# Attention with relative positions and a feed-forward layer on one core: the order of a unit's matmuls, and two orders of transfers

## What is computed

```
x = L0_attn_q                                  # 8 x 1024 x 256, 16 heads of 16
qkv = q @ in_proj_weight.T + in_proj_bias
scores = jnp.einsum('bhid,bhjd->bhij', qh, kh)
rel = jnp.clip(pos[None, :] - pos[:, None], -K, K) + K          # K = 64
bias_r = jnp.einsum('bhid,rd->bhir', qh, rel_pe)
bias = jnp.take_along_axis(bias_r, rel, axis=-1)
attn = jax.nn.softmax(scores + bias, axis=-1)
out = jnp.einsum('bhij,bhjd->bhid', attn, vh)   # then @ out_w.T + out_b
x = _layernorm(x + attention)
x = _layernorm(x + ffn(x))   # gelu(x @ bw1.T + b1) @ bw2.T + b2, hidden 1024, binarized weights
```

## Time and profile before

| | |
|---|---|
| median of 3 runs | 2308.47 us (2308.45 to 2308.74) |
| the profiled execution | 2306.05 us, its span 2304.1 us |
| busy share of the span | PE 96%, DVE 76%, ACT 68%, POOL 47% |
| granted TensorE clock | 0.982 of full speed over the span |
| projections; attention; feed-forward | about 0 to 219 us; 219 to 1960 us; 1961 to 2304 us |

### The profile page before, as it was taken

One profiled execution on the slowest core, in us unless ns is written; L12 is line 12 of the kernel. 1 busy time (PEld: TensorE's weight loads), 2 busy tenths in 40 slices (PEclk: granted clock), 3 DMA queues, 4 the chain that ended last, 5 costly groups with the idle time before them and its releaser, 6 DMA issues. The chain is left out here.

```text
span 2304.1 us, 47825 instructions
## 1 busy us (share of the span) xinstructions
PE 2213.8 (96%) x14580; PEld 1261.2 (55%) x14580; DVE 1740.0 (76%) x3447; ACT 1566.1 (68%) x2192; POOL 1086.9 (47%) x1803
## 2 busy tenths in 40 slices
PE   8997799999999999999999999999999999899997
PEld 5554355545555555555555555555555544788886
DVE  3444688888888888888888888888888884788885
ACT  3444277777777777777777777777777776577676
POOL 1000444555445554455554555545555442577763
PEclk9998599999999999999999999999999999999999
DMA  9997877777777777777777777777777771433321
GB/s 305 402 334 273 215 215 212 219 210 212 218 213 221 207 215 219 211 218 207 215 220 211 220 206 215 220 213 216 208 215 218 215 214 49 122 100 109 108 66 46
DMA packets 334570, 468.55 MB, mean 203 GB/s; under 512 B 89797, under 2 KB 262550, under 8 KB 334486
## 3 DMA queue, kind: packets, MB, share of 16 engines
q0 software_dynamic: 120960, 215.78, 34.6%
q1 hardware_dynamic: 204358, 243.32, 33.0%
q10 hardware_dynamic: 9168, 8.52, 1.1%
HBM read 244.73 MB, written 221.25 MB: 202 GB/s over the span
## 5 line engine op out<-in xcount | busy, mean ns | idle before, releaser
L1025 ACT ACTIVATE probs<-weigh_ps 128x1024 f32<-128x1024 f32 x1024 | 1047.7, 1023 | 197.3 <-PE weigh_ps L1203 188.6
L1164 PE MATMUL ring_ps<-keys,queries 48*128 48x512 f32 x2048 | 853.8, 478 | 22.0 <-DVE partial_max L1068 13.7
L1079 DVE CUSTOM_DVE_ANT_1 ring_ps<-ring_ps,band_all 128x512 f32<-128x512 f32 x1008 | 681.2, 715 | 213.6 <-PE ring_ps L1164 213.4
L1203 PE MATMUL weigh_ps<-queries,keys 50*128 50x512 f32 (+3 forms) x2688 | 748.1, 383 | 0.0
L1068 DVE TENSOR_REDUCE partial_max<-ring_ps 128x2 f32<-128x1024 f32 x512 | 627.7, 1226 | 116.2 <-PE ring_ps L1164 88.5
L1164 PEld LDWEIGHTS ring_ps<-keys,queries 48*128 48x128 f32 x2048 | 369.9, 187 | 511.7 <-issue 371.8
L1220 PE MATMUL sum_ps<-probs,values 128*32 128x512 f32 x4096 | 546.4, 605 | 0.1
L1014 ACT ACTIVATE carried<-weigh_ps 128x260 f32<-128x260 f32 (+1 forms) x512 | 211.9, 414 | 255.4 <-PE weigh_ps L1153 255.4
L925 POOL COPY carried<-carried 128x252 f32<-128x252 f32 x430 | 159.1, 395 | 458.1 <-ACT carried L1014 458.1
L1188 PE MATMUL weigh_ps<-ident,band_all 128*128 128x128 f32 x2048 | 362.5, 289 | 1.5 <-ACT carried L1014 0.6
L1203 PEld LDWEIGHTS weigh_ps<-queries,keys 50*128 50x128 f32 x2688 | 357.6, 186 | 10.4 <-issue 5.9
(11 more groups left out here) (131 smaller groups left out, 1852.9 us busy)
## 6 DMA issues: line engine op xcount, KB each, us to landing
band_scr<-carried SPq DMA_DIRECT2D x256, 512.0 KB, 6.0
band_all<-band_scr POOLq DMA_DIRECT2D x128, 512.0 KB, 5.4
band_all<-band_scr POOLq DMA_DIRECT2D x128, 256.0 KB, 4.5
keys<-k_scr POOLq DMA_DIRECT2D x128, 240.0 KB, 8.1
k_scr<-k_parts SPq DMA_DIRECT2D x16, 1792.0 KB, 9.8
queries<-q_scr POOLq DMA_DIRECT2D x128, 128.0 KB, 3.8
o_scr<-weighted_s SPq DMA_DIRECT2D x64, 256.0 KB, 8.2
keys<-k_scr POOLq DMA_DIRECT2D x128, 120.0 KB, 5.2
```

Source lines behind the costliest of these rows:

```text
L1025: nc.scalar.activation(probs[:, u % PROBS], weigh_ps[weigh_of["scores", at]][:], ACT.Exp).then_inc(s_pr, 1)
L1079: nc.vector.tensor_tensor_reduce(out=both, in0=both, in1=bias, scale=1.0, scalar=LOWEST, op0=ALU.add, op1=ALU.max, accum_out=partial_max[: ...
L1164: nc.tensor.matmul(dst, query_rows(c, h, ROWS, tile * P, (tile + 1) * P), key_rows(c, h, ROWS, c0, c0 + 512), start=True, stop=True, tile_ ...
L1203: last = nc.tensor.matmul(weigh_ps[weigh_of["scores", at]][:, h, e0 * P:e1 * P], key_rows(c, h, QROWS, k0, k0 + P), query_rows(c, h, QROWS ...
```

## The change

Three edits. In `products`, the two weighing products of a unit are written first and both looks behind them (before: look, weighing, weighing, look). In the attention stage SP's two transfers of ones are moved from the head of its program to behind the first four band writes. In the feed-forward stage, for tiles 2 and 3, SP issues the inverse ahead of the heads and the residual, and POOL's first operations are in another order.

```
-                sp.wait_ge(s_set, 5)
-                for h in range(HG):
-                    row = keys[h * ROW_TILE + ROWS:h * ROW_TILE + QROWS].bitcast(F32)
-                    sp.dma_start(...).then_inc(s_one, 16)
                 for step in range(-START, FIRST):
                     for u in range(UNITS):
+                        if step == 1 - START and u == NT:
+                            sp.wait_ge(s_set, 5)
+                            for h in range(HG):
+                                row = keys[h * ROW_TILE + ROWS:h * ROW_TILE + QROWS].bitcast(F32)
+                                sp.dma_start(...).then_inc(s_one, 16)
                         unit(0, step, u)
...
-                    if looked:
-                        look(i, n, first)
                     if step >= 0:
                         weigh(step, m, part, 1 - first)
                         weigh(step, m, part, first)
                     if looked:
+                        look(i, n, first)
                         look(i, n, 1 - first)
...
-                    if it >= 2 * EARLY:
+                    if it < 2 * EARLY:
+                        spread_inverse(sp, it, inverse_wide)
+                    else:
                         load_sums(sp, it)
                     load_heads(sp, it, heads_raw)
                     load_residual(sp, it, x_in)
                     if it >= 2 * EARLY:
                         write_inverse(sp, it)
-                    spread_inverse(sp, it, inverse_wide)
+                        spread_inverse(sp, it, inverse_wide)
...
+                skip(0)
                 divide(2)
                 residual(2)
-                skip(0)
+                divide(3)
+                skip(1)
                 for it in range(IT + 2):
                     if 0 <= it - 2:
                         add_skip(it - 2)
-                    if it + 1 < IT:
+                    if 0 < it and it + 1 < IT:
                         skip(it + 1)
-                    if it + 3 < IT:
+                    if 0 < it and it + 3 < IT:
                         divide(it + 3)
```

More of the change, by code:

```diff
@@ L835, in unit @@
                             write_bands(i, chunk)
-                sp.wait_ge(s_set, 5)
-                for h in range(HG):
-                    row = keys[h * ROW_TILE + ROWS:h * ROW_TILE + QROWS].bitcast(F32)
-                    sp.dma_start(flat(row, 0, [row.ap[0], [P, SLOTS * KCOLS // P], [1, P]]),
-                                 flat(ones[:], 0, [ones[:].ap[0], [0, SLOTS * KCOLS // P], [1, P]])
-                                 ).then_inc(s_one, 16)
                 for step in range(-START, FIRST):
                     for u in range(UNITS):
+                        if step == 1 - START and u == NT:
+                            sp.wait_ge(s_set, 5)
+                            for h in range(HG):
+                                row = keys[h * ROW_TILE + ROWS:h * ROW_TILE + QROWS].bitcast(F32)
+                                sp.dma_start(flat(row, 0, [row.ap[0], [P, SLOTS * KCOLS // P], [1, P]]),
+                                             flat(ones[:], 0, [ones[:].ap[0], [0, SLOTS * KCOLS // P], [1, P]])
+                                             ).then_inc(s_one, 16)
                         unit(0, step, u)
```

## The result

The changed kernel takes 2324.91 us (median of 4 runs, 2321.16 to 2327.96), the kernel before 2308.6 (4 runs, 2308.45 to 2309.71): ratio 1.007, 95% interval 1.0055 to 1.0085. It is slower, by 16.3 us. The forecast was 2340, with 2318 to 2358 as the range. The profiled execution is 2326.46 us, its span 2324.6, so between the two profiles the span grew by 20.5 us.

| us | before | after | difference | of this part |
|---|---|---|---|---|
| VectorE's first reduction | 239.73 | 237.52 | -2.2 | -2.2 |
| TensorE's first load of step 0 | 274.42 | 272.22 | -2.2 | 0 |
| of step 1 | 305.27 | 304.06 | -1.2 | +1.0 |
| of step 63 | 1931.01 | 1955.46 | +24.45 | +25.7 |
| feed-forward stage, first matmul | 1961.03 | 1985.48 | +24.45 | 0 |

What follows compares the result with a forecast made beforehand. The prediction took a ring between TensorE and VectorE, each waiting for the other, to bound the kernel. 2306.05 + 44 (edit 1) - 7 (edit 2) - 5 (edit 3) = 2338, or 2340 us as median; range 2318 to 2358.

Steps and rivals of the forecast that it cites:

- VectorE's late start on odd looks: Attention steps, edit 1: odd first looks end 0.25 us late per pair, lengthening the step 0.5 to 1.0 us; chance 0.63.
- more idle time in all: Profile from 600 to 1800 us: ScalarE's exponentials start earlier after TensorE, with more idle time in all.
- 0.7 us a step: Edit 1's lengthening of each attention step; in 62.5 steps +44 us, bounds +22 and +62.
- the forecast's own 0.5 to 1.0: Likeliest case: the attention step lengthens by 0.5 to 1.0 us, giving 2328 to 2358 us; chance 0.63.
- half is taken up: Rival 2: idle times re-arrange, leaving 0.35 us a step or less, 2318 and down to 2313 us; chance 0.17.
- the unrounded 0.86: Delay left per step after idle time ahead of VectorE's eight reductions covers part of 0.25 us each; taken as 0.7.
- VectorE's ring is the longer one at those same places: Reason for counting at zero the relief of the band product's wait for ScalarE, 0.32 us a step, 20 us at most.
- a later reduction holds the next odd unit's second look: Ring between TensorE and VectorE: TensorE waits for the delayed reduction, 0.05 us to spare; two of eight pairs excepted.
- The rule that I gave for the rival: Rival 3, TensorE bound, 2284 or 2287 us, chance 0.14: holds if looks load 0.25 us or more after a reduction's end.
- an unchanged 5.8: Edit 2, attention start: 5.8 us from POOL's band read issue to VectorE's first reduction, then 6.5 us earlier.
- the divide can begin some 3 us sooner: Edit 3, feed-forward start: without residual and heads ahead of the inverse, TensorE's 3.38 us wait goes almost wholly.
- what might hold it back: Edit 3's gain, taken as -5 us: VectorE's L1442, 1769 ns on average beside busy POOL, whose work now comes earlier.

Runs made afterwards that it cites:

- even and odd units apart: Kernel before with the new products order in only even units: 2307.23 against 2306.8 us, ratio 1.0003; in only odd units: 2343.17 us, ratio 1.0145.
- the short odd operation: VectorE's operation on odd looks reads 256 of 512 columns per head: 2308.11 us on the kernel before, 2282.37 us with edit 1 in all units.
- the two other kernels with this edit: Kernel before with edit 2 alone: 2304.44 us, ratio 0.9985; kernel before with edits 2 and 3: 2300.86 us, ratio 0.9971.
- the transfers alone: Kernel before with only SyncE's part of edit 3, the inverse ahead of heads and residual: 2307.16 against 2307.03 us, ratio 0.9999.
- GpSimd's order alone: Kernel before with only GpSimd's part of edit 3, first skip foremost, divide of tile 3 before the second skip: 2302.73 us, ratio 0.998.
- Two kernels that shorten one suspect each: VectorE reads half the columns, old and new order: even-look reduction 2284.0 and 2328.95 us; odd-look operation 2308.11 and 2282.37 us.

## Why the prediction was right, and what was off

**The sign and where the loss begins: right.** The loss is edit 1's, in every steady step, through VectorE's late start on odd looks: shown by the edit alone (+24.4 us), by even and odd units apart, and by the short odd operation, which turns the loss into a gain. VectorE's wait per pair was forecast at about 0.65 and came to 0.61, that before the reductions at nearly none (0.33 us a step). ScalarE was forecast to have "more idle time in all", and it has (busy 144.84 of 200 us, was 147.50). Ahead of its exponentials its idle time fell, from 129.9 to 68.3 us; ahead of the band copies its wait for the band product rose, from 184.4 to 262.2. The band product's wait and its row are gone as forecast.

**The size: 0.7 us a step was taken, 0.41 measured** (+44 against +25.7; the bounds were +22 and +62). That lies between the forecast's own 0.5 to 1.0 and the 0.35 of the rival "half is taken up", and 2325 us lies in the stated range but below the forecast's 2328 to 2358. Of 2.00 us of delay a step 1.14 was to be taken up; VectorE's waits show 1.56, and 1.16 taken up. These two figures say where the time went and not why, since VectorE's work is unchanged and they must differ by the lengthening of the step. The delay itself stands in the traces: from the first weight load of an odd unit to VectorE's start on its first look it is 0.69 us before and 0.92 to 0.93 after, in each of the eight pairs (means of steps 8 to 50). So the look is 0.23 us late where 0.25 was taken, and that is 0.15 of the 0.45 us between the unrounded 0.86 and the 0.41. VectorE's wait grew by 0.195 only, so TensorE reaches an odd unit some 0.035 us sooner after VectorE than before, 0.28 a step, and this term was put at zero. The band product's wait that went is of that size, 0.32 us a step or 0.04 a pair, and I had dropped it because "VectorE's ring is the longer one at those same places". The new order's loop runs through that band product. That its wait is what makes up the 0.035 is argued, not shown.

**The step that failed: "a later reduction holds the next odd unit's second look, which waits for it with 0.05 us to spare, and TensorE with it".** True of the old order. In the new one that look still loads 0.05 us behind the reduction in six of the eight pairs, but it isn't in the loop: the reduction can lose 0.53 us and nothing moves. The binding wait is the even unit's second look, for the odd operation. That the sum still came within the bounds is in part luck: it added up what was left of the delay behind the reductions, a path that doesn't bind, and both paths only begin with the same late look. The rule that I gave for the rival ("the time between a reduction's end and the look that waits for it") looked at the one place only. In the kernel before, the even unit's second look loads 0.05 to 0.06 us behind VectorE in three of the eight pairs and 0.10 to 0.53 behind it in five; in the new order it is 0.05 to 0.06 in seven. I had looked at none of them, and didn't ask what this slack becomes when everything ahead of it slips.

**Edit 2: 6.5 us was taken at the first reduction and 7 in the sum, 2.0 measured in the change**, outside the bounds of 3 and 9 (3.3 and 3.5 in the two other kernels with this edit). The stage's own start moves within some 4 us from run to run, so I measure from GpSimd's first key load: in the eleven profiles without the edit the first reduction comes 19.66 to 19.74 us behind it, in the three with it 17.74, 16.41 and 16.17. The steps of the estimate: the write is issued at 221.06, as forecast. It lands at 230.32, after 9.3 us; forecast were 6.0, the median, and in all eleven without the edit it takes 7.8. It now goes out between the key loads. The reads take 6.6 us from GpSimd's issue to VectorE's start, not "an unchanged 5.8". The ones beside them don't explain that: the two other kernels with edit 2 have them there as well, and take 5.3 and 5.6 us. Of the changed kernel:

```profile
221.06 4.09 SPq L807 DMA_DIRECT2D band_scr<-carried  x4
...
230.93 1.46 POOL L889 DMA_DIRECT2D band_all<-band_scr  x2 [6.97 <-DMA band_scr<-carried]
...
237.52 1.23 DVE L1069 TENSOR_REDUCE partial_max<-ring_ps 128x2 f32<-128x1024 f32 x1 [18.52 <-DMA band_all<-band_scr]
```

Against the first key load the write goes out 4.27 us earlier (1.28 us behind it, was 5.55), and 1.5 us are lost to the slower landing and 0.8 to the slower reads: 1.97, and measured is 19.70 - 17.74 = 1.96. A median over the stage was the wrong row for a transfer at its busiest moment; the 8.3 us of the same write in the earlier trace rows was the near one. The +1.0 us of step 0 goes by the clock as well: it rose to 1.00 at 286.6 us, 14.40 us into the step, and before at 287.0, 12.55 us into it, and 1.85 us more at the 1.2 GHz level cost about 0.9 us (an estimate). Edit 1 alone doesn't have it; whether edit 2, by starting the step earlier, has a part in it is open.

**Edit 3: 5 us was taken, 3.9 measured**, inside the bounds. Up to the ninth divide of the stage the lead is 5.4 us (152.6 us into the stage against 158.0). Then the kernel before wins 1.6 back at a place that the edit doesn't touch: from the ninth to the eleventh divide it takes 41.55 us, where twelve of the fourteen profiles, the changed kernel's among them, take 43.05 to 43.11. Both waits went, and the clock behind them stayed up. The reason was half right: "the divide can begin some 3 us sooner" held for 2.6 us (12.31 us into the stage before, 9.70 after), but the transfers alone are worth nothing. GpSimd's order alone brings 3.2 of the 5.4 us up to the ninth divide, and 4.3 us over the runs, against 5.4 for all of edit 3 (the intervals of the two overlap). VectorE's L1442, named as what might hold it back, took 1316 ns on average in the same 43 us of the stage against 1769:

```profile
L1446 DVE TENSOR_TENSOR hidden<-gelu,hidden 128x512 fp32r<-128x512 f32 x16 | 20.7, 1316 | 20.1 <-ACT hidden L1508 20.1
```

By the rule of the Trainium skill ("SBUF — State Buffer", section "SBUF: two separate sides") GpSimd's denser start was to cost VectorE more, and the stage to gain only 3 us. Single operations took up to 2.9 us where others took 0.69, before and after, which agrees with such a lock; that an earlier start of GpSimd would cost VectorE more does not agree.

**The total**, between the profiles, was to be +32 us and came to 20.4: the steady term 18.3 too high, edit 2 4.8 and edit 3 1.1 too favourable, and 1.0 in step 0. So 6.9 us of the error in the steady term was offset by others the other way, which is luck. The medians differ by 16.3: the profiled execution of the kernel before lies 2.6 us below its median, that of the changed kernel 1.6 above. Edit 1 cost 24.4 us, and the change without it is 0.29% faster than the kernel before.

## What to carry to other kernels

Before costing a delay in a ring of buffers, write down every wait on the ring with its slack, also the ones that have slack now; the delay picks its own binding wait, and it need not be the present one. Two kernels that shorten one suspect each, run under both orders, show which loop binds: four numbers, and they crossed here. And a wait that is shortened ahead of a fixed row of work on one engine (GpSimd's here) can come back at the end of that row; look for the next wait, and at the clock behind it. When two profiles are compared, see also whether they differ in a stretch that the edit doesn't touch: here that was 1.6 us of 3.9.

## What the runs showed of the hardware that I had not expected

In fourteen profiles the steady step repeated to 0.01 us wherever the order and VectorE's work were the same, while the first step with weighing products took anything from 30.1 to 37.6 us, by whether and for how long the clock fell back to 0.50 behind a gap in TensorE's work. In the feed-forward stage the clock fell between 13 and 30 us into it in all ten profiles with the old order of GpSimd's first operations, and in none of the four with the new. A write of 512 KB took 7.8 us to land in all eleven profiles where it stood behind the ones, and 9.0 to 9.3 where it was issued between the key loads.
